# A two-expert feed-forward layer: all experts for all tokens, or scattered slots

## The chip, the cores and the metric

The kernel runs on one core of a Trainium2 chip. The core has five engines that run side by side and meet at semaphores: TensorE (PE, matmuls and transposes), VectorE (DVE), ScalarE (ACT), GpSimd (POOL) and SyncE (SP), which here issues the plain DMAs. The metric is the device time of one execution in microseconds (us), lower is better. A comparison is made between runs on the same chip.

## What is computed

One transformer layer on 4 sequences of 512 tokens, 256 wide, in fp32: attention with 16 query and 4 key heads that adds half a softmax attention and half a gated linear attention (GLA), a layer norm, a feed-forward part with 8 experts of 176 features, and a second layer norm. The change is about the feed-forward part:

```python
router_logits = jnp.einsum('td,ed->te', x, gate_w)
routing_weights = jax.nn.softmax(router_logits, axis=-1)
top_w, top_idx = jax.lax.top_k(routing_weights, TOP_K)        # TOP_K = 2
comb = jnp.zeros((T, gate_w.shape[0]), dtype=routing_weights.dtype)
comb = comb.at[jnp.arange(T)[:, None], top_idx].add(top_w)
g = jnp.einsum('td,edf->etf', x, w_gate)
u = jnp.einsum('td,edf->etf', x, w_up)
y = jnp.einsum('etf,efd->etd', jax.nn.silu(g) * u, w_down)
out = jnp.einsum('te,etd->td', comb, y)
```

Every token has a weight other than zero for two experts of eight.

## The kernel before

**Attention.** The 16 pairs of a sequence and a key head are the groups, 0 to 15. A group has four steps c = 0 to 3, one for each 128 query tokens; the softmax part of step c covers c + 1 key blocks. Group 0 and group 15 are written out, groups 1 to 14 are one hardware loop (`Fori`). The order of each engine's instructions is written by hand in its `step`. In a step TensorE makes the scores (`score`), two small GLA matrices, the q, k, v projection of two steps ahead (`project`), the output projection of the step before (`output`), turns the softmax weights (`turn_weights`) and the next step's q and k (`turn`), and gathers the output (`gather`). VectorE takes maxima, scales the softmax (L872), subtracts the high half of a split value and adds the output into `acc`, which holds all 16 token tiles (128 tokens each) in SBUF. ScalarE does exponentials and copies out of PSUM. GpSimd turns q and k by their angle (`rotate`), weighs the features (`weigh_features`, L1227) and applies the decay (`decay`, L1239, which writes `qd`), moves V, and splits the next x. `turn` of TensorE needs `qd`. In group 15 VectorE does the decay and moves V instead.

**Precision.** fp32 matmuls against weights are done as three fp32r matmuls of high and low halves (`_hi`, `_lo`).

**Weights of the experts.** They arrive in `stage` by SyncE, in 11 pieces of 128 features (8 x 176 = 1408 = 11 x 128), and GpSimd splits them in group 15 and behind it, into the space of the attention weights. Three selection matrices come the same way.

**Feed-forward.** Token groups n = 0 to 3 of 512 tokens, pieces f = 0 to 10. `gate_up` makes 12 matmuls of 512 columns, ScalarE applies silu, `spread_comb` lays the routing weights over the 128 features by a matmul, VectorE multiplies (`multiply`), ScalarE and VectorE split h, and `down` adds 12 matmuls of 256 columns into PR. So each token goes through all 8 experts. Layer norm 1, the transposes and the routing of group n + 1 stand between the pieces of group n; of group 0, in steps 1 to 3 of attention group 15. The second norm and the store of the last token group come behind the last piece, in halves.

## Time and profile before

| | us |
|---|---|
| median of 3 runs | 1077.68 |
| lowest and highest run | 1073.81, 1077.69 |
| profiled execution | 1077.24 |
| its span | 1075.5 |
| TensorE busy | 1007.1 |
| VectorE, ScalarE, GpSimd busy | 759.4, 627.2, 633.1 |

The profile is one execution. Its span is what the traces cover; its own time has 1.7 us more. Busy time of TensorE counts overlapping matmuls once and says nothing of how well it is used; the price of a matmul is read from the distance of two starts.

### The profile page before, as it was taken

To read this page: it belongs to the slowest core of one execution; us is meant where nothing else is said; L and a number is where in the kernel's file an instruction comes from. 1 tells how busy PE (TensorE), PEld (TensorE's weight loads), DVE (VectorE), ACT (ScalarE), POOL (GpSimd) and SP (SyncE) were. 2 spreads that over 40 slices of the span, in tenths; PEclk is the share of its full clock that TensorE was granted. 3 is DMA by queue.
4 is the path that set the end of the run, shared out by engine and by line. 5 is a ranking of instruction groups with operands and counts; after the bars stand their busy time and mean duration, and the time that the engine had idled before them with its cause. 6 is when DMAs were issued, how large, how long until landed. Compare 5 with 4: busy or idle time off the path is not lost.

```text
span 1075.5 us, 20731 instructions
## 1 busy us (share of the span) xinstructions
PE 1007.1 (94%) x5860; PEld 802.7 (75%) x5860; DVE 759.4 (71%) x1741; ACT 627.2 (58%) x1944; POOL 633.1 (59%) x656
## 2 busy tenths in 40 slices
PE   4699999999999999999999999999997999999996
PEld 3567777677777777777777776777775688888886
DVE  4888767677676767676767776776769765767655
ACT  4456666666766667666666666667665334333321
POOL 5678676767666767676676767676659560202000
PEclk8899999999999999999999999999999999999999
DMA  7110000000000000000000000000002110000001
GB/s 234 50 50 25 11 10 10 10 10 15 10 10 10 10 10 10 10 11 13 10 10 10 10 10 10 10 15 10 25 0 74 58 45 1 1 21 1 20 1 40
DMA packets 26095, 24.07 MB, mean 22 GB/s; under 512 B 1744, under 2 KB 22608, under 8 KB 25936
## 3 DMA queue, kind: packets, MB, share of 16 engines
q1 hardware_dynamic: 26064, 23.67, 7.3%
q8 instruction: 17, 0.28, 0.1%
q14 instruction: 14, 0.11, 0.0%
HBM read 21.57 MB, written 2.10 MB: 22 GB/s over the span
## 4 chain that ended last, share of the span: by engine, by line
PE 79%; DVE 12%; ACT 5%; issue 3%; DMA 0%; DVEq 0%; POOLq 0%; POOL 0%; SPq 0%
PE OA L461 11%; PE S L547 11%; PE PR L362 10%; PE S L414 8%; PE S L443 6%; PE MS L434 6%; PE PR L567 6%; PE OA L452 4%; PE OA L423 4%; DVE pr L872 3%; ACT eqk L671 3%; PE PR L390 3%; PE PR L386 2%; PE MS L375 2%; DVE qd L893 2%
## 5 line engine op out<-in xcount | busy, mean ns | idle before, releaser
L644 ACT ACTIVATE pr<-S,nm 128x128 f32<-128x128 f32 (+3 forms) x256 | 131.5, 524 | 94.4 <-DVE nm L838 92.6
L1239 POOL TENSOR_TENSOR qd<-eqk,eg 128x512 f32<-128x512 f32 x56 | 68.0, 1215 | 177.9 <-issue 151.7
L461 PE MATMUL OA<-wT,V 128*128 128x512 f32 x320 | 149.3, 596 | 1.4 <-DVE wT L920 1.4
L671 ACT ACTIVATE eqk<-qkv,nmx 128x128 f32<-128x128 f32 x320 | 124.3, 395 | 8.4 <-DVE nmx L912 8.3
L1216 POOL TENSOR_TENSOR rp<-qkv,cos 128x640 f32<-128x640 f32 x64 | 100.8, 1575 | 30.9 <-ACT qkv L661 22.4
L838 DVE TENSOR_REDUCE nm<-S 128x2 f32<-128x256 f32 (+3 forms) x128 | 101.9, 818 | 21.8 <-PE S L414 20.0
L872 DVE TENSOR_SCALAR pr<-pr,rl 128x128 f32<-128x128 f32 (+3 forms) x256 | 110.2, 473 | 4.5
L461 PEld LDWEIGHTS OA<-wT,V 128*128 128x128 f32 x320 | 59.5, 190 | 72.1 <-issue 68.9
L1219 POOL TENSOR_TENSOR rp<-rp,rt 128x640 f32<-128x640 f32 x64 | 99.0, 1547 | 5.0
L1216 POOL TENSOR_TENSOR rt<-qkv,sin 128x640 f32<-128x640 f32 x64 | 98.9, 1545 | 0.0
L443 PE MATMUL S<-cm,pr 128*128 128x128 f32 x640 | 81.9, 275 | 15.7 <-DVE pr L872 15.7
L692 ACT COPY wT<-S 128x512 f32<-128x512 f32 x96 | 51.7, 592 | 67.5 <-PE S L443 67.5
L443 PEld LDWEIGHTS S<-cm,pr 128*128 128x128 f32 x640 | 71.4, 142 | 19.1 <-DVE pr L872 19.1
L362 PE MATMUL PR<-w_hi,ring_hi 128*128 (+2 forms) x256 | 78.0, 386 | 7.8 <-DVE w_lo L1131 6.9
L1227 POOL TENSOR_TENSOR eqk<-eqk,rse 128x640 f32<-128x640 f32 x56 | 72.2, 1290 | 20.8 <-PE OA L461 10.6
L763 ACT CAST wo_hi<-eqk 128x512 fp32r<-128x512 f32 x44 | 27.3, 620 | 90.2 <-DVE eqk L1096 90.2
L1310 POOL TENSOR_TENSOR rstd<-ve,neghalf 128x4 f32<-128x4 f32 x7 | 7.2, 1024 | 123.1 <-DVE ve L1031 123.1
L434 PE MATMUL MS<-wo_hi,oT_hi 128*128 (+1 forms) x256 | 74.1, 289 | 5.4 <-DVE gc L880 5.4
L362 PE MATMUL PR<-w_hi,ring_lo 128*128 (+2 forms) x256 | 73.7, 370 | 0.0
L434 PE MATMUL MS<-wo_hi,oT_lo 128*128 (+1 forms) x256 | 72.3, 282 | 0.0
L434 PE MATMUL MS<-wo_lo,oT_hi 128*128 (+1 forms) x256 | 72.2, 282 | 0.0
L547 PE MATMUL S<-ring_hi,w_hi 128*128 128x512 f32 x176 | 70.3, 399 | 0.0
(180 smaller groups left out, 2972.9 us busy)
## 6 DMA issues: line engine op xcount, KB each, us to landing
xraw<-in_x_cols SPq DMA_DIRECT2D x64, 128.0 KB, 2.2
stage<-in_wffn SPq DMA_DIRECT2D x11, 384.0 KB, 3.1
stage<-in_wqkv SPq DMA_DIRECT2D x6, 384.0 KB, 3.3
acc<-in_x_rows SPq DMA_DIRECT2D x1, 2048.0 KB, 12.6
out<-pr SPq DMA_DIRECT2D x3, 512.0 KB, 2.9
wT<-in_wo_in SPq DMA_DIRECT2D x1, 1024.0 KB, 6.5
pr<-in_wqkv SPq DMA_DIRECT2D x2, 384.0 KB, 4.0
stage<-in_wo_in SPq DMA_DIRECT2D x2, 384.0 KB, 3.2
```

The source lines that it names most:

```text
L362: last = pe.matmul(PR[:, a:b], x[:, cc, k, :], wq_cols(w, kv, k, a, b), start=(i == 0), stop=(i == len(steps) - 1))
L414: last = pe.matmul(S[:, h, 0:n], q[:, h * 128:(h + 1) * 128], k[:, 0:n], start=False, stop=(i == len(steps) - 1), skip_group_check=True)
L434: last = pe.matmul(MS[:, 0:HID], o[:, h * 128:(h + 1) * 128], r, start=(i == 0), stop=(i == len(steps) - 1))
L443: last = pe.transpose(S[:, j, h * 128:(h + 1) * 128], pr[:, h, j * 128:(j + 1) * 128], ident)
L461: last = pe.matmul(OA[:, :], V[:, j, :], wT[:, j, :], start=(c == 0 and j == 0), stop=(j == c))
L547: last = pe.matmul(S[:, 2 * q + q0 % 2, :], w[:, f, k, q, :], x[:, n % 2, k, :], start=(i == 0), stop=(i == len(steps) - 1))
L644: nc.scalar.activation(pr[:, h, 0:n], S[:, h, 0:n], ACT.Exp, bias=nm[:, h:h + 1], scale=1.0, accum_out=ls[:, h:h + 1]).then_inc(s_exp, 1)
L671: last = nc.scalar.activation(eqk[:, par, h * 128:(h + 1) * 128], qkv[:, c % C, h * 128:(h + 1) * 128], ACT.Exp, bias=nmx[:, h:h + 1], sca ...
L838: nc.vector.tensor_reduce(nm[:, 2 * pair:2 * pair + 2], S[:, 2 * pair:2 * pair + 2, 0:n], AX_X, ALU.max, negate=True).then_inc(s_nm, 1)
L872: nc.vector.tensor_scalar(pr[:, h, 0:n], pr[:, h, 0:n], rl[:, h:h + 1], None, ALU.mult).then_inc(s_pn, 1)
L1216: nc.gpsimd.tensor_tensor(to.rearrange("p (h w d) -> p h w d", w=2, d=64), src, tab, ALU.mult).then_inc(s_rt, 1)
L1219: nc.gpsimd.tensor_tensor(rp[:, c % 2, :], rp[:, c % 2, :], rt[:, :], ALU.add).then_inc(s_rp, 1)
```

## The change

**What is computed where.** Each token is copied to two slots, one for each of its experts. The slots of an expert are whole tiles of 128, so that a tile has one expert. Two sets of token tiles are handled apart: set A is the first three sequences (12 tiles, at most 31 slot tiles), set B the last (4 tiles, at most 15). All 46 (`NT`) slot tiles are always worked, empty ones too.

**Routing** (all small, in the attention groups 12 to 15 for set A, in rounds 1 to 13 of the feed-forward part for set B). Layer norm 1 of a sequence after steps k = 0, 2, 4 (statistics, VectorE) and k + 1 (scaling, GpSimd), where k counts the 16 steps of groups 12 to 15. TensorE turns two token tiles in each of steps 2 to 7 and makes their logits in fp32 a step later. VectorE ranks them, counts the tokens of each expert by a scan and TensorE by a matmul with a triangle (`prefix`), and gives each token its slot numbers `sloti` (int32) and each slot tile its expert `te`.

**Movement.** GpSimd scatters rows of `acc` to `slot_x` in DRAM by indirect DMAs, two for each token tile (`send`). SyncE loads a slot tile of 128 rows (`load_slots`) and stores its result to `slot_y` (`store_slots`); before that it writes zeros over `slot_x`. GpSimd gathers two rows for each token back (`fetch`), VectorE adds them to `acc` with their weights (`combine`), then come the statistics, GpSimd's pow, ScalarE's scaling and the store.

**A slot tile on TensorE**: `turn_x`, `gate_up` (the expert's number is read from SBUF into a register, which addresses the weights), `turn_h`, `down`, spread over three rounds by software pipelining.

**The rest.** Groups 12 to 15 are written out on every engine (`PEEL` = 12). Expert weights come whole (704 columns of gate and up, 512 of down); GpSimd splits them after the steps in `WIDE_AT`. In group 15 GpSimd keeps the decay and V. Three selection matrices, `spread_comb` and the 512-wide pieces go. The list of `jobs`, the names of buffers and the constants change with this and are left out here, as are the bodies of the routing steps.

```diff
+PEEL = NG - 4
+SETS = ((0, 3 * TPB), (3 * TPB, TILES))
+SLOT_TILES = [((b - a) * P128 * 2 + E * (P128 - 1)) // P128 for a, b in SETS]
+NT_A, NT_B = SLOT_TILES
+NT = NT_A + NT_B
...
+        WIDE_AT = (4, 5, 6, 7, 8, 9, 10, 10, 11, 12, 13, 13, 14, 14, 16, 16)
...
+        TURN_AT = {2: 0, 3: 1, 4: 2, 5: 3, 6: 4, 7: 5}
+        LOGITS_AT = {k + 1: p for k, p in TURN_AT.items()}
+        STATS_AT = {0: 0, 2: 1, 4: 2}
+        NORM_AT = {k + 1: n for k, n in STATS_AT.items()}
+        RANK_AT = {5: 0, 7: 1, 9: 2}
+        EXP_AT = {k + 1: n for k, n in RANK_AT.items()}
+        PREFIX_AT, SLOTS_AT, WEIGH_AT = 10, 11, 13
+        SEND_AT = {12: (0, 4), 13: (4, 8), 14: (8, 12)}
...
+            def load_slots(q):
+                if q == 0:
+                    sp.wait_ge(s_sent[0], 16 * 2 * MOST[0])
+                    sp.wait_ge(s_v, NU - 2)
+                    sp.wait_ge(s_rp, NU - 2)
+                    sp.wait_ge(s_gl, NU - 2)
+                if q == NT_A:
+                    sp.wait_ge(s_sent[1], 16 * 2 * MOST[1])
+                later(sp, s_tx, q - 3)
+                sp.dma_start(xg[:, q % 4, :], slot_rows(slot_x, q)).then_inc(s_xg[q % 4], 16)
+
+            def store_slots(q):
+                sp.wait_ge(s_yo, q + 1)
+                sp.dma_start(slot_rows(slot_y, q), yo[:, q % 3, :]).then_inc(s_y[q % 3], 16)
...
+            for q in range(3, NT + 3):
+                if q < NT:
+                    load_slots(q)
+                if q >= 5:
+                    store_slots(q - 5)
...
+                if not n1:
+                    turn_x(0)
+                    turn_x(1)
                 turn_weights(g, c)
+                if k in TURN_AT:
+                    pe.wait_ge(s_am, C * g + c + 1)
+                    turn_tokens(TURN_AT[k], OA)
...
+            def gate_up(q):
+                if q == 0:
+                    pe.wait_ge(s_flo, n_gu)
+                    pe.wait_ge(s_te, 1)
+                if q == NT_A:
+                    pe.wait_ge(s_te, 2)
+                expert[q] = pe.value_load(te[0:1, q:q + 1], min_val=0, max_val=E - 1)
+                pe.wait_ge(s_txh, q + 1)
+                pe.wait_ge(s_txl, q + 1)
+                later(pe, s_h, q - 1)
+                steps = [(k, x, w) for k in range(KT2) for x, w in ((xT_hi, gu_hi), (xT_hi, gu_lo), (xT_lo, gu_hi))]
+                for i, (k, x, w) in enumerate(steps):
+                    last = pe.matmul(S[:, q % 2, 0:2 * F], x[:, q % 2, k * 128:(k + 1) * 128],
+                                     expert_cols(w, expert[q], k * 2 * F, (k + 1) * 2 * F),
+                                     start=(i == 0), stop=(i == len(steps) - 1))
+                last.then_inc(s_gu, 1)
...
+                for i, (k, h, w) in enumerate(steps):
+                    rows = TAIL if k else P128
+                    last = pe.matmul(OA[:, 0:HID], h[0:rows, q % 2, k * 128:(k + 1) * 128],
+                                     expert_cols(w[0:rows], expert[q], k * HID, (k + 1) * HID),
+                                     start=(i == 0), stop=(i == len(steps) - 1))
+                last.then_inc(s_dn, 1)
...
+            for q in range(1, NT + 2):
+                if q + 1 < NT:
+                    turn_x(q + 1)
+                if q < NT:
+                    gate_up(q)
+                if q >= 2:
+                    down(q - 2)
+                if q - 1 < NT:
+                    turn_h(q - 1)
...
-                if first or last:
+                if first:
...
+            def combine(t):
+
+                a = acc[:, t, :]
+                dve.wait_ge(s_yg[t % 4], 32 * (t // 4 + 1))
+                nc.vector.scalar_tensor_tensor(out=a, in0=yg[:, t % 4, 0, :], scalar=wts[:, 0, t:t + 1], in1=a, op0=ALU.mult,
+                                               op1=ALU.add).then_inc(s_c0, 1)
+                dve.wait_ge(s_c0, t + 1)
+                nc.vector.scalar_tensor_tensor(out=a, in0=yg[:, t % 4, 1, :], scalar=wts[:, 1, t:t + 1], in1=a, op0=ALU.mult,
+                                               op1=ALU.add).then_inc(s_cb, 1)
+                dve.wait_ge(s_cb, t + 1)
+                norm_stats(2, t)
...
+            for q in range(1, NT + 2):
+                if q >= 2:
+                    h_lo(q - 2)
+                if q + 1 < NT:
+                    x_lo(q + 1)
+                if q < NT:
+                    multiply(q)
+                if q == 1:
+                    moments(3)
...
+                if k in NORM_AT:
+                    norm1(NORM_AT[k])
+                if k in SEND_AT:
+                    for t in range(*SEND_AT[k]):
+                        send(t)
+                for i in range(len(wide)):
+                    if WIDE_AT[i] == k:
+                        split_wide(i)
...
+            def send(t):
+
+                s = 0 if t < SETS[0][1] else 1
+                if t == SETS[s][0]:
+                    pool.wait_ge(s_sl, s + 1)
+                    pool.wait_ge(s_zf, 64)
+                    pool.wait_ge(s_x1a, SETS[s][1])
+                for r in range(2):
+                    nc.gpsimd.indirect_dma_start(slot_x[s], bass.IndirectOffsetOnAxis(ap=sloti[:, r, t:t + 1], axis=0),
+                                                 acc[:, t, :], None).then_inc(s_sent[s], 16)
+
+            def fetch(t):
+
+                if t == 0 or t == SETS[1][0]:
+                    for i in range(3):
+                        pool.wait_ge(s_y[i], stored(NT_A if t == 0 else NT, i))
+                later(pool, s_cb, t - 3)
+                for r in range(2):
+                    nc.gpsimd.indirect_dma_start(yg[:, t % 4, r, :], None, slot_y[0 if t < SETS[0][1] else 1],
+                                                 bass.IndirectOffsetOnAxis(ap=sloti[:, r, t:t + 1], axis=0)).then_inc(s_yg[t % 4], 16)
...
+            for g in range(PEEL, NG):
+                for c in range(C):
+                    step(g, c, last=g == NG - 1, k=C * (g - PEEL) + c)
+            split_wide(14)
+            split_wide(15)
+            norm1(3)
+            for t in range(3 * TPB, TILES):
+                send(t)
+            for t in range(3 * TPB):
+                fetch(t)
+                if t >= 3 and t % 2:
+                    rs2((t - 3) // TPB, ((t - 3) % TPB) // 2)
+            rs2(2, 1)
+            for t in range(3 * TPB, TILES):
+                fetch(t)
+            rs2(3, 0)
+            rs2(3, 1)
```

**Order on TensorE, feed-forward part.** Before, the last three of the twelve gate and up matmuls of a piece (four times the same three), then the first three of the twelve of a down-projection:

```order
858 L547 MATMUL S<-ring_hi,w_hi 128x512
859 L547 MATMUL S<-ring_hi,w_lo 128x512
860 L547 MATMUL S<-ring_lo,w_hi 128x512
861 L567 MATMUL PR<-wo_hi 128x256 [waits s_hlo,s_hhi]
862 L567 MATMUL PR<-wo_lo,wo_hi 128x256
863 L567 MATMUL PR<-wo_hi,wo_lo 128x256
```

After, the first half of one slot tile's gate and up matmuls, and ahead of it the transposes of h (L673, L674), those of the next slot tile (L650) and the register load (L659):

```order
1655 L673 MATMUL S<-cm,rp 128x128 [waits s_hl,s_h]
1656 L674 MATMUL S<-cm,rp 48x128
1657 L650 MATMUL PR<-cm,qkv 128x128 [waits s_txl,s_xg3]
1658 L650 MATMUL PR<-cm,qkv 128x128
1659 L659 TENSOR_LOAD te
1660 L659 ISA x2
1661 L665 ISA [waits s_h,s_txl,s_txh]
1662 L665 MATMUL S<-w_hi,ring_hi 128x352
1663 L665 REGISTER_ALU
1664 L665 MATMUL S<-w_lo,ring_hi 128x352
1665 L665 MATMUL S<-w_hi,ring_lo 128x352
```

The 512-column matmuls with fixed weights have become 352-column ones with weights addressed by a register that is loaded just ahead.

**Order on TensorE, last attention step.** Before, from the last output matmuls (L434) over the transposes of the softmax weights (L443) to the first of the router's (L524):

```order
656 L434 MATMUL MS<-wo_hi,oT_lo 128x256
657 L434 MATMUL MS<-wo_hi,oT_hi 128x256
658 L434 MATMUL MS<-wo_lo,oT_hi 128x256
659 L434 MATMUL MS<-wo_hi,oT_lo 128x256
660 L443 MATMUL S<-cm,pr 128x128 [waits s_pn]
661 L443 MATMUL S<-cm,pr 128x128 x15
662 L524 MATMUL PR<-ring_hi,gate_hi 128x512 [waits s_jlo,s_xlo]
```

After, from the last output matmuls (L535) to the transposes of the softmax weights (L544); `xg` (in `qkv`) is where a slot tile is loaded:

```order
1285 L535 MATMUL MS<-wo_hi,oT_lo 128x256
1286 L650 MATMUL PR<-cm,qkv 128x128 [waits s_rql,s_qdT,s_xg0]
1287 L650 MATMUL PR<-cm,qkv 128x128
1288 L650 MATMUL PR<-cm,qkv 128x128 [waits s_rql,s_qdT,s_xg1]
1289 L650 MATMUL PR<-cm,qkv 128x128
1290 L544 MATMUL S<-cm,pr 128x128 [waits s_pn]
1291 L544 MATMUL S<-cm,pr 128x128 x15
```

The transposes of the first two slot tiles, which wait for their loads (s_xg0, s_xg1), now stand ahead of those of the weights (L544).

**Order on GpSimd, step 0 of group 15.** Before, rotation, then splits of expert weights, then the next rotation:

```order
137 L1219 TENSOR_TENSOR rp<-rp,rt 128x640 [waits s_rt]
138 L1273 TENSOR_SCALAR gate_hi<-stage 128x2x8 [waits s_job1]
139 L1280 TENSOR_TENSOR gate_lo<-stage,gate_hi 128x2x8 [waits s_jhi]
140 L1273 TENSOR_SCALAR w_hi<-stage 128x512 [waits s_job0,s_op,s_proj]
141 L1280 TENSOR_TENSOR w_lo<-stage,w_hi 128x512 [waits s_jhi]
142 L1273 TENSOR_SCALAR wo_hi<-stage 128x256
143 L1280 TENSOR_TENSOR wo_lo<-stage,wo_hi 128x256 [waits s_jhi]
144 L1273 TENSOR_SCALAR w_hi<-stage 128x512 [waits s_job1,s_op,s_proj]
```

After, the same step with the scatters:

```order
272 L1402 TENSOR_TENSOR eqk<-eqk,rse 128x640 [waits s_re,s_o,s_cp]
273 L1423 COPY V<-qkv 128x128
274 L1414 TENSOR_TENSOR qd<-eqk,eg 128x512 [waits s_trk,s_eg,s_wf]
275 L1418 TENSOR_TENSOR qd<-eqk,eg 128x128
276 L1391 TENSOR_TENSOR rp<-qkv,cos 128x640 [waits s_trk,s_rp,s_cp]
277 L1391 TENSOR_TENSOR rt<-qkv,sin 128x640
278 L1394 TENSOR_TENSOR rp<-rp,rt 128x640 [waits s_rt]
279 L1503 DMA slot_x<-acc,sloti 3968x256 [waits s_x1a,s_zf,s_sl]
280 L1503 DMA slot_x<-acc,sloti 3968x256 x7
281 L1453 TENSOR_SCALAR w_hi<-stage 128x704 [waits s_proj,s_job0]
282 L1455 TENSOR_TENSOR w_lo<-stage,w_hi 128x704 [waits s_fhi]
283 L1402 TENSOR_TENSOR eqk<-eqk,rse 128x640 [waits s_re,s_o,s_cp]
```

Weighing, V and decay are back in this group (L1402 to L1418), and eight scatters stand between the rotation of step 0 and the weighing of step 1; eight more follow in each of the next two steps.

## Rows read from the trace of the kernel before

**Rows 1.** The page, part 1: busy time, share of the span, instructions.

```profile
PE 1007.1 (94%) x5860; PEld 802.7 (75%) x5860; DVE 759.4 (71%) x1741; ACT 627.2 (58%) x1944; POOL 633.1 (59%) x656
```

**Rows 2.** Table by stretches: us; busy us (instructions) per engine, TensorE clock, DMA.

```profile
649.30:801.30 152.00, 147.12 (x876) 114.67 (x874) 108.34 (x258) 103.23 (x342) 106.00 (x108) 1.00 0.04 12
801.30:858.90 57.60, 48.02 (x274) 36.97 (x272) 49.23 (x116) 27.84 (x86) 41.14 (x46) 0.97 0.21 61
858.90:1067.60 208.70, 207.19 (x1184) 180.93 (x1182) 131.51 (x276) 70.11 (x112) 32.91 (x32) 1.00 0.04 14
```

**Rows 3.** TensorE in order of time: start us, us, instruction; first scores of groups 12, 15.

```profile
649.33 1.11 PE L414 MATMUL S<-k0T,rqT 128*128 128x128 f32 x8
...
801.55 1.11 PE L414 MATMUL S<-k0T,rqT 128*128 128x128 f32 x8
```

**Rows 4.** TensorE in order of time: transposes in group 14, then one feed-forward piece.

```profile
794.19 1.91 PE L443 MATMUL S<-cm,pr 128*128 128x128 f32 x16
795.94 0.60 PE L386 MATMUL PR<-cm,rp 128*128 128x128 f32 x4
...
872.39 0.40 PE L547 MATMUL S<-ring_hi,w_hi 128*128 128x512 f32 x1
872.63 0.40 PE L547 MATMUL S<-ring_hi,w_lo 128*128 128x512 f32 x1
...
875.19 0.28 PE L567 MATMUL PR<-wo_hi 128*128 128x256 f32 x1
...
876.63 0.40 PE L555 MATMUL MS<-w_hi,w_lo 128*128 128x512 f32 x1
```

**Rows 5.** Groups by line and form: busy us, mean ns; idle before, releasers.

```profile
L692 ACT COPY wT<-S 128x512 f32<-128x512 f32 x96 | 51.7, 592 | 67.5 <-PE S L443 67.5
...
L903 DVE SCALAR_TENSOR_TENSOR acc<-MS,acc 128x256 f32 x56 | 23.6, 421 | 53.4 <-PE MS L434 53.4
```

**Rows 6.** GpSimd's smallest split (ns min/median/max); DMA issues, median us to landing.

```profile
L1273 POOL TENSOR_SCALAR gate_hi<-stage x1: 204/204/204, 811.7 to 811.7; 128x16 fp32r<-128x16 f32 x1
...
xraw<-in_x_cols SPq DMA_DIRECT2D x64, 128.0 KB, 2.2
```

**Rows 7.** Groups by line and form, GpSimd: rotate, weigh, split of 768 columns, norm1, pow.

```profile
L1219 POOL TENSOR_TENSOR rp<-rp,rt 128x640 f32<-128x640 f32 x64 | 99.0, 1547 | 5.0
...
L1227 POOL TENSOR_TENSOR eqk<-eqk,rse 128x640 f32<-128x640 f32 x56 | 72.2, 1290 | 20.8 <-PE OA L461 10.6 <-DVE rse L955 10.2
...
L1304 POOL TENSOR_SCALAR acc<-acc,mv,rstd 128x256 f32<-128x256 f32 x16 | 21.0, 1324 | 17.7 <-DVE qkv L1038 17.7
...
L1280 POOL TENSOR_TENSOR w_lo<-stage,w_hi 128x768 fp32r<-128x768 f32 x6 | 11.8, 1970 | 0.5
...
L1310 POOL TENSOR_TENSOR rstd<-ve,neghalf 128x4 f32<-128x4 f32 x7 | 7.2, 1024 | 123.1 <-DVE ve L1031 123.1
...
L1273 POOL TENSOR_SCALAR w_hi<-stage 128x768 fp32r<-128x768 f32 x6 | 5.1, 856 | 0.5 <-DMA stage<-in_wqkv 0.5
```

**Rows 8.** GpSimd in order of time, group 14: the waits ahead of qd, in brackets.

```profile
754.40 1.10 POOL L1239 TENSOR_TENSOR qd<-eqk,eg 128x512 f32<-128x512 f32 x1 [1.95 <-ACT eg L654]
...
766.11 1.29 POOL L1239 TENSOR_TENSOR qd<-eqk,eg 128x512 f32<-128x512 f32 x1 [1.61 <-issue]
...
779.46 1.09 POOL L1239 TENSOR_TENSOR qd<-eqk,eg 128x512 f32<-128x512 f32 x1 [4.25 <-issue]
...
793.34 1.37 POOL L1239 TENSOR_TENSOR qd<-eqk,eg 128x512 f32<-128x512 f32 x1 [5.00 <-issue]
```

**Rows 9.** TensorE in order of time, group 15: after the gap, idle time in brackets.

```profile
834.46 0.38 PE L434 MATMUL MS<-wo_hi,oT_hi 128*128 128x256 f32 x1 [3.61 <-DVE gc L880]
...
836.28 0.41 PE L434 MATMUL MS<-wo_hi,oT_hi 128*128 128x256 f32 x1
```

**Rows 10.** VectorE in order of time, group 14: four equal scalings, two by two.

```profile
765.45 0.62 DVE L872 TENSOR_SCALAR pr<-pr,rl 128x256 f32<-128x256 f32 x2
...
766.18 1.79 DVE L872 TENSOR_SCALAR pr<-pr,rl 128x256 f32<-128x256 f32 x2
```

939 lines of the change are left out of this document (493 added, 446 removed).

## The prediction

> **What bounds the kernel now.** I read the page first: TensorE is busy for 94% of the span, far ahead of the others [rows 1]. Then the table by stretches, which splits the span where the work changes [rows 2]: groups 12 to 14 of the attention (TensorE 147.1 of 152.0 us), group 15 (48.0 of 57.6) and the feed-forward part (207.2 of 208.7); a tail of 7.9 us follows. With what stands before 649.1 us that is the whole span. The first scores of groups 12 and 15 start at 649.33 and 801.55, three groups apart, so a group takes 50.74 us [rows 3], and TensorE sets them. The feed-forward part is TensorE alone: 44 pieces (11 feature tiles by 4 token groups), at full clock.
>
> The price of a matmul is the distance between two starts, not its duration, because they overlap. 512 columns of fp32r: 0.24 us (872.39 to 872.63). 256 columns: twelve in 1.44 us, 0.12 each (875.19 to 876.63). A 128-column fp32 transpose: sixteen in 1.75 us, 0.11 each (794.19 to 795.94) [rows 4].
>
> **Feed-forward part: the arithmetic.** A piece of before is 12 matmuls of 512 columns, 12 of 256 and one that spreads the weights: 2.8 + 1.4 + 0.24 = 4.5 us, times 44 = 196, with the routing between 208.7. A slot tile of after is 2 transposes in, 6 matmuls of 352 columns (0.16 each between 0.12 and 0.24), 2 transposes of h, 6 of 256 columns: 0.22 + 0.96 + 0.22 + 0.72 = 2.12 us. There are 46, whatever the routing gives, in 47 rounds: 100 us. So about half of TensorE's work in this part goes, and the question is what spoils 100 us.
>
> First the chain between engines. h is turned at the end of a round and must be read by ScalarE and subtracted by VectorE before the down-projection of the next, which has 0.22 + 0.96 us of other matmuls in front of it. 256 columns cost VectorE 0.42 us; on ScalarE, whose 512 columns take 0.59, I take 0.39 [rows 5]. ScalarE has the y copy ahead of it: 0.39 + 0.39 + 0.42 and about 0.2 for hand-overs is 1.4 us, against 1.18: 0.2 us is exposed, a round of 2.3 us. ScalarE's four operations (1.55 us) and VectorE's three (1.2 us) fit.
>
> Second, each tile's expert number is loaded from SBUF into a register of TensorE before its gate and up matmuls. No row of before shows such a read. It lies between nothing and 2.2 us, the landing of the smallest frequent DMA [rows 6], the only row here of something fetched through memory. When it starts, TensorE still has two pairs of transposes and some of the down matmuls queued, about 0.7 us. I take the middle, 1.1 us, which is 0.4 us over that cover: a round of 2.7 us. At 2.2 us it would be 2.1 + 1.5 = 3.6 us. The Trainium skill ("DMA: Bandwidth & Descriptors", Latency and other measured facts) gives such a tensor load a floor of about 600 ns; no row here shows it, and by it alone the round would stay near 2.3 us and the total would be 1028 us.
>
> 47 rounds of 2.7 are 127 us. In front stand gate_up(0) and the last output, 3 us. Beside them set B's moments, routing and slots go through VectorE (some 11 us in rounds 1 to 13, where it has 1.5 us free in each) and ScalarE changes its table for one exp: 5 us exposed. Behind them is a new tail, since the last tiles must go out and come back: y copy 0.5, store 2.4, eight gathers one after another on GpSimd at s each, landing 2.0, two weighted adds and statistics 1.35, the rest of the norm, with GpSimd's pow, 1.7, normalising 0.8, the output DMA 2.2 [rows 6] and hand-overs 0.2. That is 11.2 + 8s.
>
> The price s of an indirect DMA on GpSimd carries the rest. Before has none. Below lies GpSimd's smallest operation that reads a stage, 0.20 us, and above the 2.2 us of a DMA's whole way [rows 6]. GpSimd has to make 128 row addresses, which is more like the 128x256 work of 0.4 to 1.3 us than like the smallest; I take 1.3. The tail is 21.6 us, and the part is 3 + 127 + 5 + 22 = 157 us, against 216.6 from 858.9 to the end.
>
> **Groups 12 to 14, peeled.** TensorE gets 24 transposes (2.6 us), 24 matmuls of 8 columns (taken at 0.14 each, a little over a transpose, 3.4 us) and three small ones: 6.4 us. VectorE gets about 20 us in pieces of 2 to 3; it is idle for 29% of the stretch [rows 2], and I count 2 us as exposed. GpSimd gets norm1 after steps 1, 3 and 5, each a pow of 1.0 and four of 1.32, 6.5 us with gaps, and weight splits of 704 columns (2.7 us) and 512 (1.95), read from those of 768 [rows 7]. Its cover is how long it waits before qd: 1.6, 4.25 and 5.0 us in the steps of group 14 [rows 8], and TensorE needs qd about 1 us later. Set against it, norm1 after step 1 leaves 1.3 us, that after step 3 2.5, and that of step 5 with its split 5.0; the other splits fit. So 9 us. Together 17 us, the stretch 169 us.
>
> **Group 15.** Before, it had 57.6 us with stalls, as VectorE also does the decays there: 3.6 us before the output matmul, for example [rows 9]. Now GpSimd does them again, and this removes those stalls; what is late next is GpSimd itself. Its queue from the group's start: weigh, V and decay end at 5.1, as qd in step 0 of group 14 does [rows 8]; rotate 4.7 (three of 1.55 [rows 7]); eight scatters 8s; split 2.7; weigh to decay 3.3 (L1227 1.3, V and qd 2.0); rotate 4.7; 8s; two splits 3.9; weigh to decay 3.3. The last qd is ready at 28 + 16s. Then 8s again, 2.2 until the last scatter has landed and 2.2 for the first slot load. TensorE waits for that load in turn_x(0), **ahead** of turn_weights(15, 3), and behind it come 6 us of transposes and gather. The group takes 38.4 + 24s = 69.6 us, 12 more than before. At s = 0.8 it would be level.
>
> A rule speaks against the scatters being here. VectorE's own row shows the port being shared: two 256-column scalings took 0.62 us and the next two 1.79 us, beside GpSimd at work [rows 10]. The Trainium skill ("SBUF — State Buffer", SBUF: two separate sides) says that a VectorE operation in a two-port mode locks GpSimd out while it writes descriptors. By it, if every third of the 24 scatters waited out one 0.9 us scaling (half of the 1.79), they would take 7 us more; this lies inside my range for s.
>
> **The sum.** 649.1 + 169 + 69.6 + 157 = 1044.9 us of span. The profiled execution took 1077.24 us for a span of 1075.5, so 1.7 lies around it: 1046.6, **1047 us**. The median of the three runs is 1077.68, 0.4 above the profiled one, so the same comparison holds: 2.9% faster.
>
> **Rivals.**
> *Scatter and gather are dear (slower).* One mechanism: s of 2 us or more on GpSimd. Every 1 us of s costs 24 in group 15 and 8 in the tail, and from s = 1.35 on the gathers of set A no longer keep up with a round: two of them per combine, which stands in VectorE's queue ahead of the next tile's x_lo and multiply, 12 times. At 1.9 it costs 19 + 13 = 32 us and the gain is gone; at 2.2, 29 + 20, giving **1096**. For it: the whole way of a DMA is 2.2, and descriptors of 128 rows are made by a processor. Against it: issuing is only part of that way. 0.15.
> *TensorE's clock falls (slower).* The output matmuls behind the 3.61 us gap of group 15 came 0.20 us apart (ten from 834.46 to 836.28) instead of 0.12 [rows 9]: level 1.2 GHz instead of 2.4. If the rounds, with TensorE idle for a fifth of each, ran so, they would take 4.0 us: **1108**. Against it: the gaps are ten times shorter, and the stretch of groups with idle time stays at 1.00. 0.05.
> *Register read dear.* 2.2 us, rounds of 3.6: **1089**. 0.07.
> *Both unknowns cheap.* Read hidden, rounds of 2.3, s = 0.7: 19 + 19 off, **1009**. 0.25.
> *The gain is lost in the peeled groups.* VectorE's additions and the small waits cost 25 us more: **1072**, no change. 0.08.
> That fewer matmuls don't do what they say is no rival: the tile count is fixed. The forecast, with s from 1.0 to 1.6 and rounds of 2.5 to 3.0, has 0.40.
>
> **The numbers.** About 0.5% (1072 to 1083) is what a measurement can tell from no change. Faster: 0.40 + 0.25 and most of the no-change case's lower half, 0.73; same 0.08; slower 0.15 + 0.05 and most of the read case, 0.19. Leaving out 1 in 10 at each end gives 1008 to 1096.
>
> **What would show it.** In the profile of after: starts of the gate matmuls 2.7 us apart in the rounds; a gap of 0.4 us ahead of each first one, put down to TensorE's sequencer; GpSimd's DMA instructions 1.3 us apart; group 15 near 70 us with TensorE waiting for the slot load; 22 us from the last matmul to the end; the granted clock at 1.00 throughout the rounds. I am wrong if the scatters come over 1.9 us apart, if the rounds take over 3.3 us, or if groups 12 to 14 grow by over 30 us.

## The result, and the profile after

The changed kernel takes **1092.39 us** (median of four runs, 1087.87 to 1096.06) where the kernel before takes 1077.68 beside it: a ratio of 1.0135, 95% interval 1.0102 to 1.0168. It is slower by 1.35%, and the forecast was 2.9% faster. The time lies inside the range of 1008 to 1096, but the sign is wrong, and that it lies inside is luck: the upper end stood for dear scatters, and they turned out as cheap as forecast.

Three stretches of the profiled execution of after (1093.5 us, span 1091.7), as the table by stretches gives them: groups 12 to 14, group 15, and the rounds of the feed-forward part up to the last matmul. They answer to [rows 2].

```profile
core 0: us, PE busy (x) PEld busy (x) DVE busy (x) ACT busy (x) POOL busy (x), PEclk, DMA share, GB/s
649.50:842.80 193.30, 170.45 (x956) 133.76 (x955) 134.52 (x327) 106.94 (x351) 142.67 (x140) 0.92 0.16 50
842.80:922.96 80.16, 53.58 (x259) 40.22 (x258) 40.53 (x93) 27.01 (x84) 55.38 (x55) 0.81 0.22 72
922.96:1069.20 146.24, 135.18 (x776) 111.89 (x774) 77.19 (x242) 69.67 (x196) 45.20 (x47) 0.92 0.36 106
```

From the last matmul to the end are 22.5 us more (1069.2 to 1091.7). Set against before and against the forecast, in us:

| stretch | before | forecast | after |
|---|---|---|---|
| up to group 12 | 649.1 | 649.1 | 649.5 |
| groups 12 to 14 | 152.2 | 169 | 193.3 |
| group 15, up to the first gate matmul | 57.6 | 69.6 | 80.2 |
| feed-forward part with its tail | 216.6 | 157 | 168.7 |

So the part that was rewritten did give back 48 us. The attention groups beside which the routing and the scatters were put took 64 of them: 41 in groups 12 to 14, and 23 in group 15. The error of 47 us is made of 24 in groups 12 to 14, 11 in group 15 and 12 in the feed-forward part. The prediction had said that it would be wrong if groups 12 to 14 grew by over 30 us; they grew by 41.

In groups 12 to 14 TensorE waits where it hardly waited before. The waits of TensorE from 700 to 845 us, largest first:

```profile
PE OA L524 <- DVE oT_lo L948: 15.5, 4, 5.5
PE MS L476 <- DVE gl L1076: 3.2, 2, 2.8
```

The numbers are the time in all, how often, and the longest. oT_lo is the low half of a step's attention output, gl the gate logarithms of a later step. (A fifth wait at L524, 3.20 us, ends at 848.47 in group 15.) The longest ends at 809.31. What VectorE did ahead of it, in order of time; the line numbers are those of the changed kernel:

```profile
801.90 0.70 DVE L1076 SCALAR_TENSOR_TENSOR gl<-qkv,lnp 128x128 f32<-128x128 f32 x1 [0.69 <-ACT lnp L793]
802.53 0.17 DVE L1119 TENSOR_REDUCE small<-lg 128x4 f32<-128x32 f32 x1
...
803.54 1.89 DVE L1130 TENSOR_TENSOR rk<-lg 128x256 f32<-128x256 f32 x1
805.46 1.36 DVE L1131 TENSOR_TENSOR rk<-rk,tri 128x256 f32<-128x256 f32 x1
806.86 0.42 DVE L1133 TENSOR_TENSOR rk<-rk 128x256 f32<-128x256 f32 x1
...
808.39 0.26 DVE L1144 TENSOR_TENSOR before<-run,picked 128x96 f32<-128x96 f32 x1
808.57 0.68 DVE L948 TENSOR_TENSOR oT_lo<-OA,oT_hi 128x512 fp32r<-128x512 f32 x1
```

The next step's scores began at 801.25. The routing block stands at the end of the step before in VectorE's queue, 6.0 us of it, and oT_lo is behind it. TensorE's queue has the gla matmul (L524), which overwrites OA and so waits for oT_lo, ahead of the gate sums (L476) and the projection. Two operations of the block also took 1.89 and 1.36 us where the same shape took 0.42 just behind them; GpSimd had a weight split (1.82 us) and a weighing (1.43 us) beside these two.

In group 15 the three longest waits are for GpSimd and for the first slot tile:

```profile
873.88 1.11 PE L491 MATMUL PR<-cm,qd 128*128 128x128 f32 x4 [9.04 <-POOL qd L1418]
895.56 1.06 PE L491 MATMUL PR<-cm,qd 128*128 128x128 f32 x4 [5.12 <-POOL qd L1418]
914.26 1.11 PE L650 MATMUL PR<-cm,qkv 128*128 128x128 f32 x4 [7.18 <-DMA qkv<-slot_x]
```

The last of these is not the scatters' alone. SyncE's queue, in order of time:

```profile
908.19 3.04 SPq L392 DMA_DIRECT2D stage<-in_wdn  x2
911.41 4.36 SPq L407 DMA_DIRECT2D qkv<-slot_x  x6
```

The last scatter had landed at 907.02. The first slot load was issued at 911.41, 4.4 us later, since two loads of expert weights stand ahead of it in SyncE's queue, and the second of them (issued at 910.90) waits for a split that GpSimd does behind its scatters.

The two unknown prices can be read. GpSimd's scatters (32, with landing) and their spacing, and TensorE's reads of the expert number (46; load, two register operations):

```profile
L1503 POOL DMA_INDIRECT slot_x<-acc,sloti x32: 956/960/1232, 858.1 to 980.7; - x32
...
DMA to landing us min/median/max: 2.4/2.4/3.6
```

```profile
862.20 0.96 POOL L1503 DMA_INDIRECT slot_x<-acc,sloti  x1 [0.30 <-issue]
863.47 0.96 POOL L1503 DMA_INDIRECT slot_x<-acc,sloti  x1 [0.30 <-issue]
```

```profile
L659 PEldq TENSOR_LOAD <-te x46: 295/301/527, 919.7 to 1057.2; - x46
L659 PEldq FUSED_REGOPS  x46: 151/151/165, 920.2 to 1057.5; - x46
L659 PEldq SEQ_ASSERT  x46: 18/18/23, 920.5 to 1057.7; - x46
```

A scatter is 0.96 us long and 1.27 from start to start. A read is 0.30 + 0.15 + 0.02 us. Rounds 18 to 35 (the first is number 0) are 2.51 to 2.71 us long, 2.60 in the mean, with TensorE at full clock and hardly idle; the first gate matmuls of two rounds:

```profile
987.17 0.43 PE L665 MATMUL S<-w_hi,ring_hi 128*128 x1
...
989.74 0.43 PE L665 MATMUL S<-w_hi,ring_hi 128*128 x1
```

But the first 16 rounds take 56 us and not 42. Four of these rounds show what the clock can do to them. Rounds 10 to 13 in this profile, and below it in that of a later run of the same kernel (a_third):

```profile
961.86:973.44 11.58, 11.02 (x74) 9.34 (x72) 7.79 (x33) 5.43 (x17) 1.48 (x2) 1.00 0.32 96
961.26:979.24 17.98, 17.98 (x74) 16.12 (x72) 8.69 (x36) 5.65 (x17) 2.83 (x3) 0.53 0.24 74
```

The same matmuls take 11.6 us at a granted clock of 1.00 and 18.0 at 0.53. In a_third TensorE had waited 1.9 and 1.3 us in the two rounds ahead, the clock then fell to its lower level (1.2 GHz), and TensorE was busy for the whole of the 18 us.

### The profile page after: what moved, and what is told of

It reads as the page before. It is cut to its first block, busy times and chain, and to the rows that moved or that the text cites. A ratio compares the mean times of both kernels' runs of the same rounds, so it can differ in the third digit from the quotient of the medians.

```text
span 1091.7 us, 20493 instructions
## 1 busy us (share of the span) xinstructions
PE 963.3 (88%) x5516; PEld 755.1 (69%) x5516; DVE 724.8 (66%) x1756; ACT 634.1 (58%) x2044; POOL 705.4 (65%) x721
## 4 chain that ended last, share of the span: by engine, by line
PE 66%; DVE 15%; ACT 7%; POOL 5%; issue 5%; DMA 1%; DVEq 0%; ACTq 0%; SPq 0%; POOLq 0%
PE PR L463 9%; PE OA L562 9%; PE S L515 7%; PE S L544 6%; PE MS L535 6%; PE OA L686 5%; PE S L665 4%; ACT eqk L780 4%; PE OA L524 4%; PE OA L555 3%; DVE pr L990 3%; PE PR L491 2%; PE PR L487 2%; POOL slot_x L1503 2%; DVE gl L1076 2%
## 5 line engine op out<-in xcount | busy, mean ns | idle before, releaser
L1414 POOL TENSOR_TENSOR qd<-eqk,eg 128x512 f32<-128x512 f32 x59 | 71.9, 1219 | 182.4 <-issue 161.9
L544 PE MATMUL S<-cm,pr 128*128 128x128 f32 x640 | 84.0, 280 | 12.1 <-DVE pr L990 12.1
L1402 POOL TENSOR_TENSOR eqk<-eqk,rse 128x640 f32<-128x640 f32 x59 | 75.9, 1287 | 21.5 <-DVE rse L1073 12.2
L524 PE MATMUL OA<-qdT,kdT 128*128 128x512 f32 x128 | 69.8, 628 | 18.8 <-DVE oT_lo L948 18.7
L544 PEld LDWEIGHTS S<-cm,pr 128*128 128x128 f32 x640 | 73.7, 145 | 15.0 <-DVE pr L990 15.0
L535 PE MATMUL MS<-wo_hi,oT_hi 128*128 (+1 forms) x256 | 76.0, 297 | 4.7 <-DVE gc L998 4.2
L463 PE MATMUL PR<-w_hi,ring_lo 128*128 (+2 forms) x256 | 76.5, 382 | 0.0
L535 PE MATMUL MS<-wo_hi,oT_lo 128*128 (+1 forms) x256 | 73.0, 285 | 0.0
L535 PE MATMUL MS<-wo_lo,oT_hi 128*128 (+1 forms) x256 | 72.9, 285 | 0.0
L463 PE MATMUL PR<-w_lo,ring_hi 128*128 (+2 forms) x256 | 70.6, 358 | 0.0
L515 PE MATMUL S<-KT_hi,rq_hi 128*128 128x256 f32 (+2 forms) x192 | 68.9, 359 | 0.0
```

The source lines that it names most:

```text
L463: last = pe.matmul(PR[:, a:b], x[:, cc, k, :], wq_cols(w, kv, k, a, b), start=(i == 0), stop=(i == len(steps) - 1))
L515: last = pe.matmul(S[:, h, 0:n], q[:, h * 128:(h + 1) * 128], k[:, 0:n], start=False, stop=(i == len(steps) - 1), skip_group_check=True)
L524: pe.matmul(OA[:, :], kdT[:, :], qdT[:, c % 2, :], start=True, stop=True).then_inc(s_at, 1)
L535: last = pe.matmul(MS[:, 0:HID], o[:, h * 128:(h + 1) * 128], r, start=(i == 0), stop=(i == len(steps) - 1))
L544: last = pe.transpose(S[:, j, h * 128:(h + 1) * 128], pr[:, h, j * 128:(j + 1) * 128], ident)
```

## The experiments

Theory 1, formed on this trace: the loss in groups 12 to 14 is VectorE's routing blocks ahead of oT_lo, made larger by the half clock behind each gap. Its rivals: the writing out of the groups, the amount of added work wherever it stands, GpSimd's splits, the clock alone. The kernels of one set ran on one chip. That turned out to matter, so times are compared inside a set, and the steps of the attention across sets only where the difference is large. The first and the second set have no run of the changed kernel; where the first is set against it, the numbers are those of the result, from another set. Between its profiles groups 12 to 14 of the changed kernel vary from 190.6 to 193.3 us.

### First set: what groups 12 to 14 lose

**e1_peel**, the kernel before with

```diff
-            with pe.Fori(1, NG - 1) as g:
+            with pe.Fori(1, NG - 4) as g:
...
+            for g in range(NG - 4, NG - 1):
+                for c in range(C):
+                    step(g, c)
```

and the same on the four other engines.

> The kernel before, with groups 12 to 14 written out behind the loop as the changed kernel has them, and nothing else changed. Theory 1 (the 41 us that groups 12 to 14 lost are VectorE's routing blocks, which stand ahead of oT_lo, and the half clock behind each gap): writing the groups out is free, 1077 us, within 2 us of before. Rival (unrolled code has to be fetched and each step starts late): groups 12 to 14 grow by over 10 us, 1088 us or more. The steps of group 12 of the changed kernel ran at their old lengths for two steps, which speaks for the first.

Measured 1077.44 us, 1.0007 of before (0.9993 to 1.0020). Its groups 12 to 14:

```profile
649.70:801.60 151.90, 147.43 (x878) 114.96 (x877) 109.49 (x258) 103.25 (x342) 106.36 (x108) 1.00 0.05 13
```

Written out as straight-line code, the three groups cost nothing. That rival falls.

**e2_drip**, the changed kernel with the blocks turned into pieces:

```diff
+                drip(k, 0)
                 if first and c == 0:
                     wo_low(0)
                 else:
                     add_output(g - 1 if c == 0 else g, C - 1 if c == 0 else c - 1)
...
+                drip(k, 1)
                 if n2 and c:
                     log_gates(g, c + 2)
...
-                if k in RANK_AT:
-                    route_rank(RANK_AT[k], 2 * RANK_AT[k] + 2)
...
+                drip(k, 2)
```

where drip issues the next one to five operations from a table by step and place, and the exponential of the logits (ScalarE) moves one step up.

> The changed kernel with VectorE's routing work the same but handed out in one to four operations at a time: ahead of add_output, ahead of log_gates and at the end of each of steps 4 to 13, and the tables in the same steps as before or one later. Theory 1 (the blocks delay oT_lo, TensorE's in-order queue waits for it, and its clock halves behind the gap): the gaps ahead of the gla matmul (18.7 us in five steps) go, and some of the clock's loss with them: groups 12 to 14 from 193 to 165 us, the whole 1065 us (1060 to 1072). Rival 2 (it is the amount of added work on VectorE, GpSimd and TensorE, wherever it stands): 1088 to 1096 us, as the changed kernel. Rival 3 (the clock falls for another reason, such as what TensorE does in the steps): gaps gone but 1080 us.

Measured 1076.53 us (0.9996 of before, 0.9978 to 1.0014), 16 less than the changed kernel took. Groups 12 to 14, and two of TensorE's waits from 700 to 845 us, which takes in the first 16 us of group 15 (line numbers have moved; L554 is the gla matmul):

```profile
651.40:829.20 177.80, 162.53 (x956) 128.10 (x955) 139.05 (x328) 106.62 (x351) 143.51 (x140) 0.97 0.18 54
```

```profile
PE MS L506 <- DVE gl L1106: 5.8, 3, 2.8
PE OA L554 <- DVE oT_lo L978: 2.5, 1, 2.5
```

With the same operations VectorE is busy for longer than in the changed kernel (139.1 us against 134.5), and yet the stretch is 15.5 us shorter once they stand apart. Where they stand, and in what pieces, is what counts, and the rival of the mere amount falls as the whole cause. But 26 us of the 41 stay, where I expected 13.

**e3_double**, the five comparisons of each block done twice in place (`rank_again(RANK_AT[k])` ahead of `route_rank`).

> The changed kernel with the comparison part of each of the three routing blocks (five operations, about 3.5 us as they ran in groups 13 and 14) done twice at the same place, at the ends of steps 5, 7 and 9. Theory 1: each block already ends after oT_lo is wanted, so every added microsecond is a longer gap: 3 x 3.5 = 10.5 us and some clock on top, 1105 us (1100 to 1112). Rival (VectorE's additions are hidden and something else sets the steps): no more than 3 us, 1092 to 1095.

Measured 1101.57 us (1.0219, 1.0190 to 1.0249), 9 more than the changed kernel; the wait at the gla matmul is 22.5 us where it was 15.5. The time is as theory 1 says, at its lower end. Not all of the 9 us lie there, though: in the profiles groups 12 to 14 take 198.0 us and not 193.3, and the first 16 rounds, which this edit doesn't touch, 59.8 and not 56.4.

**e4_behind**, TensorE's order in steps 6, 7, 10 and 11:

```diff
-                if c:
+                inside = k is not None and k >= 5 and c >= 2 and n2
+                if c and not inside:
                     gla_matrix(g, c)
...
+                    if inside:
+                        project(g, c + 2, lambda: gla_matrix(g, c), at=5)
```

> The changed kernel with one order on TensorE changed in steps 6, 7, 10 and 11: the gla matmul, which waits for oT_lo, stands inside the projection of the step after next (10 of its 12 matmuls ahead of it) and not ahead of it. Theory 1: the gaps ahead of it in steps 6, 10 and 11 (4.4, 5.5 and 2.9 us) shrink by the 1.7 us to 3 us of projection that runs in them, 5 to 7 us together, less if VectorE's mask and what follows come later for it: 1086 us (1082 to 1092). Rival (the gap is not what costs, the rest of the step is as late anyhow): 1092, unchanged.

Measured 1102.23 us (1.0225, 1.0194 to 1.0257): both theories miss, it is 10 **slower**. TensorE's waits from 700 to 845 us say why:

```profile
PE MS L476 <- DVE Ut L978: 13.4, 3, 5.8
PE MS L476 <- DVE gl L1079: 3.2, 2, 2.8
...
PE OA L524 <- DVE oT_lo L951: 2.6, 1, 2.6
```

Next in TensorE's queue were the gate sums, which wait for Ut (part of the GLA state), and Ut stands directly behind oT_lo in VectorE's queue. The wait only changed its name. That the gla matmul, with all that VectorE makes of it, came later on top is my reading of the 10 us and not shown. A late block on VectorE could not be passed here by another order on TensorE, since what TensorE would do instead needs what is behind that block too.

### Second set: group 15 and the register read

**e5_turn** is e2_drip with `turn_x(0)` and `turn_x(1)`, and what ScalarE and VectorE do with them, behind `gather` of the last step.

> The version with VectorE's routing handed out in pieces (e2_drip, 1076.5 us), and one more edit: the first two turn_x of the feed-forward part stand behind the last gather of step 15 and not ahead of its turn_weights, where TensorE waited 6.2 us for the first slot tile. Theory (a true wait of the last step): the last step loses those 6 us, but the first round then waits for the same tile, and GpSimd has only the sends and the last splits ahead of it: 1072 us (1069 to 1076). Rival (the end of the last splits or of the sends sets the first round anyway): 1076, unchanged.

**e6_send** is e5_turn with

```diff
-        SEND_AT = {12: (0, 4), 13: (4, 8), 14: (8, 12)}
+        SEND_AT = {12: (0, 1), 13: (1, 3), 14: (3, 12)}
```

> e5_turn with the 24 scatters spread otherwise over GpSimd's steps 12, 13 and 14: 2, 4 and 18 in place of 8, 8 and 8. Theory (in group 15 GpSimd is the bound, and 8 scatters of 1.27 us ahead of a step's decay are what TensorE waits for, 9.9 and 7.7 us): 7.6 us less in step 13 and 5 less in step 14, while step 15 hides the rest only up to its own 13 us, so 1065 us (1060 to 1070). Rival (the splits and the attention work of GpSimd fill the group by themselves and the scatters only move): 1072, as e5_turn.

**e7_static** is the changed kernel with `expert[q] = (q * E) // NT` in place of the load.

> The changed kernel with the expert of each of the 46 rounds fixed when it is built, so that TensorE reads no number and addresses nothing by a register; the outputs of tiles with another expert are wrong. Theory (a read of 0.30 us with its 0.15 and 0.02 us is hidden behind queued matmuls): 1090 to 1093, unchanged. Rival (the read or the addressing costs in each round): 46 x 0.47 = 22 us less, 1070.

**e8_early** is e5_turn with the loop ended four groups earlier, the first two batches routed in groups 8 to 11, and other tables.

> e5_turn with groups 8 to 11 written out too, the routing of the first two batches done there, the third batch's in groups 12 to 14 with the tables ready a step and a half earlier, VectorE's pieces only where it waits in the kernel before, and the scatters at 4, 4, 2, 4, 10 over steps 10 to 14 of the last 16. Theory (what is left in groups 12 to 15 is the additions' density: VectorE, GpSimd and the clock behind each gap): groups 12 to 14 near 160 us, group 15 near 66, the whole 1050 us (1042 to 1060). Rival (each added operation costs its time on TensorE's path wherever it stands): 1070 or more.

Measured 1095.70 (1.0158), 1087.74 (1.0104), 1100.22 (1.0229) and 1093.67 us (1.0153). None of the four times can be set against its expectation, because in all of them rounds 15 and 16 (in e7_static 16 and 17) and the rounds from 36 on took up to 9.2 us each, which no kernel of the first set showed. Their steps can be read all the same:

- e5_turn: the wait for the slot load in the last step gives way to one of 5.2 us for pr (the softmax weights), and the first gate matmul starts at 906.3, where e2_drip has 905.8. Nothing gained.
- e6_send: steps 13 and 14 take 15.5 and 17.6 us, where e5_turn has 24.9 and 22.0: the scatters ahead of the decay were what TensorE waited for. But then 18 scatters stand ahead of V of the last step:

```profile
895.44 2.07 PE L592 MATMUL OA<-wT,V 128*128 128x512 f32 x2 [12.36 <-POOL V L1572]
```

- e7_static: rounds 20 to 34 take 2.47 to 2.48 us, where the other three have about 2.60.
- e8_early: groups 12 to 14 take 171.1 us and group 15 66.9, but groups 8 to 11, 203.0 before, now 217.7. From the start of group 8 to the first gate matmul it takes 455.7 us, e5_turn 459.5. Spreading moves the loss and brings 4 us, so this part of my theory fell.

### Third set: the same kernels on one chip, and the clock

**a_again**, **e2_again**: nothing changed.

> The changed kernel once more, on the chip that runs the other three of this set, since four versions that ran together on one chip (e5_turn to e8_early) each showed two stretches of 7 to 9 us in the feed-forward rounds, at its scatters and at its first gathers, that no version on the other chip had. If those stretches belong to the chip, this kernel gives 1092 or 1100 here, and the comparison inside this set holds either way; if they belong to the moved turn_x and the fixed experts, it gives 1092.

> e2_drip once more, for the same reason: 16 us under the changed kernel on the same chip by theory 1 (13 to 19), whatever the chip; by the rival that the first comparison was one of two chips, under 5 us.

Measured 1110.65 us (1.0281, 1.0249 to 1.0313) and 1098.79 us (1.0193, 1.0170 to 1.0216). So the stalls go with the chip, or with something else that differs between the sets: the kernel that took 1092 in one takes 1111 in another, where before takes 1077 in both. Pieces save 12 us here, 10.7 of them in groups 12 to 14 (190.6 against 179.9).

Where the 18 us are: in the profile of a_again rounds 15 to 17 take 17.3 us and rounds 35 to 38 take 20.5, where the changed kernel had 7.7 and 11.1. ScalarE at round 36, with GpSimd's gathers beside it:

```profile
1043.41 0.37 ACT L857 CAST ring_hi<-PR 128x256 fp32r<-128x256 f32 x1 [1.08 <-remote]
1048.44 0.32 ACT L862 ACTIVATE qd<-S 128x176 f32<-128x176 f32 x1 [4.66 <-remote]
1049.22 0.37 ACT L872 COPY eqk<-OA 128x256 f32<-128x256 f32 x1 [0.46 <-remote]
```

```profile
1037.65 0.99 POOL L1513 DMA_INDIRECT pr<-slot_y,sloti  x1 [54.79 <-DMA slot_y<-eqk]
...
1046.46 0.95 POOL L1513 DMA_INDIRECT pr<-slot_y,sloti  x1 [0.30 <-issue]
```

TensorE stood still from 1045.8 to 1050.5 us. The gate and up matmuls for which ScalarE's SiLU (L862) waits had ended at 1045.8, and so had VectorE's product of the round before; yet it ran at 1048.44, a microsecond after the eighth gather in a row had ended. A part of each stall is the clock: rounds 16 and 37 come behind the longest one and take 4.38 us each at a granted 0.50.

**e9_fill**, the changed kernel with unread transposes in front of six waits:

```diff
+                for _ in range(FILL.get(k, 0)):
+                    pe.transpose(PR[:, 512:640], k0T[:, :], ident)
                 later(pe, s_oTl, u)
```

> The changed kernel with transposes that nobody reads put on TensorE just ahead of six of its waits (34, 44 and 22 of 0.11 us ahead of the gla matmul in steps 6, 10 and 11; 70 and 36 ahead of the turn in steps 13 and 14; 15 ahead of the first down), each shorter than the wait it stands in. Theory (the half clock behind a gap is caused by the gap: about 9 us of groups 12 to 14, 6 of group 15 and 3 of the rounds): the same waits end at the same time, the clock stays at its full level behind them, and 10 to 18 us go: 1078 (1074 to 1084). Rival (the clock falls for another reason, or the waits set everything): 1092, or later by whatever the fillers overrun.

Measured 1107.29 us (1.0275, 1.0251 to 1.0300), against 1110.65: within the intervals the same. Groups 12 to 14 and group 15, of e9_fill, then of a_again:

```profile
649.00:836.30 187.30, 175.43 (x1055) 139.99 (x1054) 134.25 (x327) 106.59 (x351) 142.97 (x140) 0.96 0.17 51
836.30:915.80 79.50, 61.83 (x365) 50.42 (x364) 40.56 (x93) 27.01 (x84) 55.73 (x55) 0.87 0.23 73
```

```profile
650.80:841.40 190.60, 169.86 (x955) 133.53 (x954) 132.84 (x327) 107.01 (x351) 142.90 (x140) 0.92 0.16 50
841.40:921.90 80.50, 53.41 (x259) 39.34 (x258) 39.01 (x93) 27.02 (x84) 55.26 (x55) 0.83 0.22 72
```

The granted clock rises from 0.92 to 0.96 and from 0.83 to 0.87, and the stretches shrink by 3.3 and 1.0 us. So the gaps do cause the half clock, and what the fillers gave back of it was worth about 4 us, where I had given it 15. They gave back half of what was missing in groups 12 to 14 and a quarter in group 15, so the price of the rest isn't shown. My reading is that VectorE and GpSimd, whose chains do not run faster for it, set the steps that have gaps; TensorE's wait for the first slot load indeed grew from 6.2 to 8.8 us.

**e10_mix**, e5_turn with `SEND_AT = {12: (0, 1), 13: (1, 3), 14: (3, 7), 15: (7, 12)}`.

> e2_drip with the first two turn_x behind the last gather, and the scatters at 2, 4, 8 and 10 in GpSimd's steps 12 to 15 in place of 8, 8, 8 and 0; the last 10 stand behind V of the last step, on which TensorE waited 12.4 us in e6_send. Theory (GpSimd's order in group 15): steps 13 and 14 as in e6_send (15.5 and 17.6 us), the last step without the wait for V, and then only the slot tiles to wait for: 8 to 14 us under e2_drip on the same chip. Rival (the sum of GpSimd's work in group 15 sets the first round, whatever the order): within 3 us of e2_drip.

Measured 1088.34 us (1.0094, 1.0070 to 1.0118), 10.5 under e2_again. The first gate matmul starts at 900.5 and not at 907.5, and group 15 takes 70.8 us and not 76.6. Theory, against the rival of a fixed sum: the order in GpSimd's queue is worth about 6 us in group 15. It holds two things that no run separates. The decays of steps 13 and 14 come sooner, and the last splits now stand ahead of the last ten scatters, so that no load of weights holds up the first slot load in SyncE's queue. Where the rest of the 10.5 lies isn't shown.

### Fourth set: pacing, splits, and all together

**a_third** (unchanged), and **e11_pace**, with a wait on the rounds' count ahead of each indirect DMA of the last batch and of each of the first four gathered tiles:

```diff
+                    if s:
+                        pool.wait_ge(s_gu, 14 + 2 * (t - SETS[1][0]) + r)
                     nc.gpsimd.indirect_dma_start(slot_x[s],
...
+                if t < 4:
+                    pool.wait_ge(s_gu, 34 + t)
```

> The changed kernel as the measure of this set, since it took 1092 us on one chip and 1111 on another: 1092 or 1111 here, by whether ScalarE is held up while GpSimd issues its indirect DMAs in the rounds.

> The changed kernel with GpSimd's indirect DMAs of the feed-forward part held apart: the 8 scatters of the last batch one for each round from round 14 on, and the first 4 gathered tiles one for each round from round 34 on, in place of 8 in a row each time. Theory (on a chip where the rounds stall, ScalarE's instructions come 1 to 5 us late while GpSimd issues such DMAs back to back, and it is the row of them that does it): the stall of 8 us at rounds 15 and 16 goes, the one at round 36 becomes a few small ones, 8 to 14 us less than the changed kernel on the same chip. Rival (each indirect DMA costs ScalarE the same wherever it stands): no gain. On a chip without the stalls: unchanged within 3 us by both.

This chip doesn't stall: 1093.16 us (1.0135, 1.0086 to 1.0185) and 1095.48 us (1.0179, 1.0144 to 1.0214), the same as expected for it. It tells nothing of the cause. The trace does tell what the edit did. The scatters of the last batch come 2.5 to 2.7 us apart and not 1.27, but the first eight gathers still 1.25 to 1.30: two of them per round is their pace anyhow, so the waits ahead of the gathers hold nothing apart.

**e12_unsplit**, e2_drip with `WIDE_AT = (16,) * 16`: no expert weight is split before the last step is over, and all but the first two loads of them wait for the last step as well. It was run once, and only its steps are read.

> e2_drip with none of the 16 splits of expert weights in steps 4 to 15: all stand on GpSimd behind the last step, with their loads, which makes the whole some 45 us longer; only the steps are read. Theory (the 26 us that groups 12 to 14 still lose once VectorE's blocks are broken up come from VectorE and from TensorE's added work): steps 4 to 11 stay within 3 us of e2_drip's, and group 15, where GpSimd is the bound, gets 10 to 14 us shorter. Rival (GpSimd's splits stretch VectorE's work beside them or delay the decay): groups 13 and 14 lose 8 us or more of what is left.

Its groups 12 to 14:

```profile
652.70:823.90 171.20, 162.74 (x955) 128.19 (x954) 129.78 (x328) 106.71 (x351) 126.11 (x123) 0.97 0.13 41
```

That is 6.6 us less than e2_drip and 8.7 less than e2_again, and steps 13 and 14 are 8 us shorter than in e2_drip (21.7 and 18.3 against 24.4 and 23.6). My figure of 3 us was wrong: GpSimd's splits with their loads, for which I had counted the cover as enough, cost 7 to 9 us in groups 12 to 14. TensorE itself waited for GpSimd for only 0.2 us there, so they act through VectorE or ScalarE; by which operation isn't shown.

**e13_best**, e10_mix with the paced DMAs and the moments of the first and third batch ahead of `add_output` in steps 0 and 4.

> e10_mix (1088 us, 22 under the changed kernel on its chip) with the paced DMAs of e11_pace, and the moments of the first and third batch where VectorE waits for the output projection in steps 0 and 4 in place of the step's end. Theory: 22 us for e10_mix's edits, up to 3 for the moments (a wait of 2.8 us for gl in step 5 goes), and e11_pace's 8 to 14 on a chip that stalls: 1076 there, 1065 to 1070 on a chip that doesn't. Rival (the gains overlap): 1085 or more where it stalls, 1075 or more where it doesn't.

Measured **1067.75 us** (0.9923, 0.9896 to 0.9951): faster than the kernel before. Its three stretches, up to the first gate matmul and to the end of the rounds:

```profile
648.70:824.10 175.40, 162.22 (x955) 127.63 (x954) 137.64 (x328) 107.08 (x351) 144.16 (x140) 0.97 0.18 55
824.10:895.50 71.40, 50.27 (x259) 38.49 (x257) 45.47 (x94) 27.82 (x86) 56.58 (x55) 0.85 0.24 77
895.50:1040.00 144.50, 131.10 (x774) 109.13 (x774) 76.26 (x242) 68.59 (x195) 45.16 (x47) 0.95 0.37 109
```

Against the changed kernel on the same chip (a_third: 192.1, 80.6 and 149.7 us) it gains 17 us in groups 12 to 14, 9 in group 15 and 5 in the rounds; those 5 are the difference of rounds 10 to 13, which ran at 0.53 in a_third and at 0.87 here. Its first slot load is issued 0.02 us after the last scatter of set A has landed.

### Fifth set: the read's price

**e13_again** (e13_best unchanged) and **e14_static** (e13_best with the experts fixed as in e7_static).

> e13_best once more, with more rounds and beside its twin: 0.992 of the kernel before (0.988 to 0.996), 1067 to 1070 us, on a chip without the stalls at GpSimd's DMAs; 1.000 to 1.010 on one with them.

> e13_best with the expert of each round fixed when it is built, so that TensorE reads no number for it; the outputs of tiles with another expert are wrong. e7_static could not tell the read's price, since its set ran on a chip with the stalls and had no changed kernel beside it. Theory (the read of 0.30 us with its 0.15 and 0.02 us is hidden): 46 rounds of 2.6 us as in e13_again, at most 0.1 us a round less for the first matmul of each round, so within 5 us. Rival (the read holds the queue in each round): 46 x 0.47 = 22 us less.

Measured 1077.22 us (1.0000, 0.9981 to 1.0019) and 1068.89 us (0.9913, 0.9890 to 0.9937). This chip stalls at the gathers, which still come 1.25 us apart with one exception: rounds 36 to 38 of e13_again take 3.7, 5.3 and 3.5 us. Its rounds 15 and 16 take 2.6 and 2.7 us, where the unpaced kernels of the second and third set took 5.4 to 8.9 and 4.0 to 4.6 there (e7_static one round later). So holding the eight scatters apart seems to have taken that stall away; no run has the unpaced kernel on this chip, and chips differ. The first matmul of two rounds that follow one another, of e13_again and then of e14_static:

```profile
961.94 0.42 PE L697 MATMUL S<-w_hi,ring_hi 128*128 x1
...
964.54 0.42 PE L697 MATMUL S<-w_hi,ring_hi 128*128 x1
```

```profile
962.51 0.41 PE L699 MATMUL S<-w_hi,ring_hi 128*128 128x352 f32 x1
...
964.99 0.41 PE L699 MATMUL S<-w_hi,ring_hi 128*128 128x352 f32 x1
```

In the mean of rounds 18 to 35 it is 2.60 us a round with the read and 2.47 without: 0.12 us each, 5.6 us over 46 rounds, of 0.47 that the read is long. It is the price of the read together with the addressing by its register, and e7_static shows the same two lengths. The whole is 8.3 us shorter; where the other 2.7 lie I can't say, and the intervals of the two ratios leave room for them.

## Why the prediction was wrong

**The failed step** is that of the peeled groups, and in it the sentence "VectorE gets about 20 us in pieces of 2 to 3; it is idle for 29% of the stretch [rows 2], and I count 2 us as exposed." An average idle share hides nothing by itself. VectorE's largest waits from 650 to 801 us in the kernel before:

```profile
DVE rse L955 <- ACT eqk L671: 11.7, 9, 1.6
DVE acc L903 <- PE MS L434: 11.6, 9, 1.9
DVE gl L958 <- ACT lnp L684: 7.8, 12, 0.7
```

The idle time lies in single waits of up to 1.9 us, ahead of rse (a reciprocal that GpSimd's weighing needs), the output's add and gl. The blocks, up to 6 us long, were put where there is hardly any: at a step's end, ahead of oT_lo. Taking them apart gives back 10.7 (e2_again) to 15.5 us (e2_drip), and twice the comparisons at those places made the wait for oT_lo 7.0 us longer (e3_double). The rival "the gain is lost in the peeled groups" named this mechanism at 25 us and 0.08; groups 12 to 14 came out 24 us over the forecast.

**GpSimd's share there** was 9 us, for norm1 and one split, with "the other splits fit". By e12_unsplit the splits cost 7 to 9 us. Of the 41 us, then, some 11 to 15 are VectorE's blocks and 7 to 9 the splits; at least 3 are the clock behind gaps (e9_fill), and these overlap with the first. What is left is e12_unsplit's 171.2 us against 152.2, 19 us. TensorE's own work is 9.4 of them: by the distances of starts in the changed kernel the 24 transposes take 3.0 us, the logits, 48 matmuls in the trace where the prediction counted 24, take 5.8, and the small ones 0.6, where the forecast had 6.4 in all. norm1 and what is left of VectorE's density make the other 10; these I didn't separate. They follow the work: e8_early moved it and groups 8 to 11 grew by 14.7 us.

**Group 15** had its chain right and was sized low: 69.6 against 80.2, and with the measured s of 1.27 the forecast would have been 68.9. The 11.3 us between are three things. GpSimd's last qd was ready 52.7 us after the group's start and not 48.3, because it waited 4.1 us ahead of the first decay and 1.4 ahead of the rotation behind it; this was while TensorE waited 3.20 us for oT_lo, behind VectorE's table work. The first slot load was issued 4.4 us after the last scatter had landed, behind two loads of weights in SyncE's queue, a term that the prediction didn't have. And from its landing to the first gate matmul it took 8.7 us and not 6, at the lower level of the clock: sixteen transposes come 0.21 us apart, against 0.11 in [rows 4]. TensorE's wait of 7.2 us for the load is the one that was named, but taking it away brought nothing (e5_turn), since pr was late too.

**The rounds.** "A round of 2.7 us" was 2.6, by two errors that nearly cancel, which is luck: the read was to expose 0.4 us and costs 0.12; the round without it was to be 2.3 and is 2.47. The rounds with what stands in front of and beside them were to take 135 us (3 + 127 + 5) and took 146. Rounds 0 to 14 hold the difference: they take 53.9 us where fifteen of 2.60 are 39. In e9_fill the same rounds ran at full clock throughout:

```profile
915.82:966.81 50.99, 44.08 (x285) 37.09 (x284) 25.28 (x89) 23.56 (x61) 13.66 (x13) 1.00 0.23 71
```

So some 3 us of the 15 are the clock (0.84 in the changed kernel's profile), and 12 are not. Of these TensorE's own transposes, logits and counts for set B are 3.2 by their starts, and the prediction had left them out; the rest stands beside set B's moments and routing on VectorE and isn't separated. On the clock the rival was half right. A round at the lower level takes 4.38 us (round 11 of a_third, granted 0.50; 2.46 at 1.00 in the changed kernel's profile), which is the 4.0 of the rival and more, but only some of the rounds run so. That the clock would stand at 1.00 throughout the rounds was wrong: it was 0.92. The tail was 22.5 against 21.6.

Two sums of the prediction are slightly off, and nothing hangs on them: its four terms give 1044.7 us and not 1044.9, and twelve times 0.24 is 2.9, which makes the 44 pieces of before 201 us and not 196.

On the two rules that the prediction weighed: the Trainium skill ("DMA: Bandwidth & Descriptors", Latency and other measured facts) gives a tensor load a floor of about 600 ns; here the load is 0.30 us in the trace, 0.47 with its register operations, and the measurement decides. By the Trainium skill ("SBUF — State Buffer", SBUF: two separate sides) VectorE's two-port work would have held up descriptor writing. In this trace the scatters of group 15 run 1.27 us apart in the middle and 1.26 to 1.54 within the rows of eight, VectorE's scalings beside them; all that exceeds 1.27 adds up to under 1 us, so the 7 us don't appear. What is stretched is VectorE beside GpSimd's other work: 1.89 and 1.36 us in place of 0.42 in group 14.

**What stays open.** Why ScalarE's instructions come late on some chips while GpSimd issues indirect DMAs in a row. The stalls go with the chip or the set, they coincide with rows of eight such DMAs, and where the scatters were spaced theirs didn't appear; a cause the runs don't show. In the traces of those sets the transfers to and from the two slot tensors carry no landing time, and in the others they do (2.2 us for a load), which may point to where these tensors lie; that wasn't tried. Nor was a kernel in which the first slot load stands ahead of the last loads of weights and nothing else is changed, or one that holds the gathers apart.

## What to carry to other kernels

Before you put work beside a bound engine, find the single waits that it will fill, with their place in the queue, and size each piece to its wait; a share of idle time is no cover. Ask of each queue, that of the DMAs included, what stands directly behind the added block, and who waits for that: here the same operations made the kernel 1.35% slower as blocks at a step's end and, in pieces, with the scatters reordered and the moments moved, 0.8% faster on one chip and level on another. When the bound engine then shows gaps, reordering it doesn't help if its next items need the same late engine.

## What the hardware showed that I had not expected

- The price of the half clock depends on who sets the pace. In groups 12 to 14 raising it from 0.92 to 0.96 brought 3.3 us of 190; in four rounds that TensorE fills, the same work took 11.6 us at 1.00 and 18.0 at 0.53. Executions of one kernel differ in which rounds it strikes.
- TensorE can read a number from SBUF into a register and address its weights by it for 0.12 us a round.
- An indirect DMA of 128 rows of 1 KB holds GpSimd for 1.27 us, and lands after 2.4 us as a scatter and 3.1 us as a gather.
- The same kernel differs by 18 us between sets on different chips (1092 and 1111), mainly in two stretches beside GpSimd's indirect DMAs, while the kernel before, which has none, takes 1076 to 1078 on each.
